# Cross-attention with its score products on 64-row halves of the array, and scores and values issued in one step

## The chip, the cores and the metric

The kernel runs on one core of a Trainium2 chip. The metric is the time of one execution in microseconds of the device. All data are fp32; some operands are held as fp32r, a form that TensorE multiplies in one pass.

## What is computed

A decoder of two layers over 32 sequences of 112 tokens (width 256), with a context of 375 tokens (width 192) for each sequence. Each layer has a self-attention block, a cross-attention block and a mixture of experts; x is normalised ahead of each and the result is added to it. The change touches the cross-attention of both layers, which is, for layer 0:

```python
q = x @ Wq.T + bq                       # 16 heads of 16
k = context @ Wk.T + bk
v = context @ Wv.T + bv
attn = jnp.einsum('bihd,bjhd->bhij', q, k) * SCALE
attn = jax.nn.softmax(attn, axis=-1)
out = jnp.einsum('bhij,bjhd->bihd', attn, v)
out = out.reshape(B, NQ, IN_DIM)
return out @ Wo.T + bo
```

Layer 1 has no product with Wo: out is added to x as it is.

## The kernel before

The stages run one after the other, with a barrier between them. `cross_attention` is called once for each layer. It goes through 8 groups of 4 sequences, and through each sequence in 4 units of 4 heads; a group has 16 units. The first and the last group are written out, the six between are one loop on every engine.

**Operands.** Each head has 16 numbers, and q and k are each held as a high and a low part in fp32r, so the product of one head needs 64 rows: q stands there as high, high, low, low and k against it as high, low, high, low. `kP` holds a pair of heads in one piece of 128 rows, head k of the pair (k is 0 or 1) on rows 64k to 64k + 63. `qP[:, s, k]` is the query of head k alone: its own 64 rows are filled by DMA, and the 64 of the other head are zeros, set once by POOL. So a product over 128 rows gives the scores of one head. One more column of k holds an identity, from which the row is shifted later.

**A unit u** goes through these steps, each on the engine named:
- `score` (PE, L1276), for each of its 2 pairs: two matmuls, 112 queries x 376, each into a bank of its own (0 and 1 for pair 0, 2 and 3 for pair 1). It waits until the maxima of the same pair of the unit before are read.
- `neg_max` (DVE, L1495), for each pair: the negative row maxima out of two banks.
- `make_diag` (POOL, L1433): the maxima of the 4 heads as diagonals.
- `exponent` (PE, L1290 and L1292), in 3 steps c = 0, 1, 2 of 125 context tokens each: the maxima are put in (L1290), and then the scores are computed again, turned (two matmuls of L1292). It writes bank 4 or 5 in turns, and waits until the exponential of the step two before is done.
- `exp` (ACT, L1389): one exponential for each step.
- `values` (PE, L1308): 12 matmuls (24 records) on 32-column parts of the array, 3 for each of the 4 heads, into bank 6.
- `copy_o4` (ACT, L1397): bank 6 to memory; the values of the next unit wait for it.

**The order** is written out by hand on every engine. Step i of a group is step c = i mod 3 of unit i // 3, and step `at` = i mod 12 of its sequence. Scores run two units ahead (`AHEAD`). On PE the steps before are: exponent, then a score pair of unit u + 2 (c = 0 and 1) or the values of unit u - 1 (c = 2). The jobs of a sequence are put behind the step that the table `AT` names: "xT" (two transposes of the normalised x, L1252, copied by ACT, L1382), "q" (the projection, L1258, which waits for that copy; then DVE splits it and DMA lays it out), "back" (four transposes of a finished sequence's output, L1321, then DVE divides by the row sums), and in layer 0 "oT" (two transposes, L1329, copied by ACT, L1402) and "y" (the product with Wo, L1335, which waits for that copy). All of them use bank 7, one after the other. ACT and DVE go through the same steps with their own part of each.

```python
    AT = {"xT": 1, "q": 2, "back": 4, "oT": 7, "y": 8}
```

Of the kernel before, what the change touches and what calls it, by code (L numbers as in the profile page):

```python
# [20 lines left out]
P = 128  # L21
EPS = 1e-5
GROUP = 4
ONE = 1
# [1077 lines left out]
def cross_attention(e, layer):  # L1102

    nc, sem, psum, bank, x, mv, rstd, ident, d = e.nc, e.sem, e.psum, e.bank, e.x, e.mv, e.rstd, e.ident, e.d
    T, D, B, NG, KD, H, HD = e.T, e.D, e.B, e.NG, e.KD, e.XH, e.XD
    KB, NJ, NKV = e.KB, e.NJ, e.NKV
    HU, SU, HALF = e.XU, e.SU, e.HALF
    a = e.xa[layer]
    n_ = f"x{layer}_"
    ST = (bank[4], bank[5])  # L1110
    PV, JOB = bank[6], bank[7]
    NU = GROUP * SU
    SS = SU * NJ
    VW, VH = P // HU, e.VH
# [2 lines left out]
    F32R = mybir.dt.float32r  # L1117
    AHEAD = 2
    RING = 4
    AT = {"xT": 1, "q": 2, "back": 4, "oT": 7, "y": 8}  # L1120
    SLOT = {at: j for j, at in AT.items()}
    MAKE = ("xT", "q")

    with ExitStack() as st:
# [14 lines left out]
        qP = sb("qP", [P, GROUP, 2, PAIRS, T], F32R)  # L1139
        kP = sb("kP", [P, 2, PAIRS, NKV + 1], F32R)  # L1140
# [8 lines left out]
        if layer == 0:  # L1149
            oT = sb("oT", [P, KD, T])  # L1150
# [8 lines left out]
        s_ps, max_done, diag_ready = count("scores_ps"), count("max_done"), count("diag_ready")  # L1159
# [5 lines left out]
        def since(g, per_group, n):  # L1165

            return max(g * per_group + n, 0) if type(g) is int else g * per_group + n
# [9 lines left out]
        with nc.Block() as block:  # L1177
# [62 lines left out]
            def _(pe):  # L1240
# [18 lines left out]
                                                 xnT[:, k, :], start=(k == 0), stop=(k == KD - 1))  # L1259
                        last.then_inc(q_ps, 1)  # L1260

                def score(g, u, pair):

                    if u >= NU:
                        g, u = g + 1, u - NU
                    s, q = divmod(u, SU)
                    r = s % 2
                    n = 2 * u + pair
                    if pair == 0 and q % 2 == 0:
                        pe.wait_ge(k_loaded[q // 2][r], g * (32 * GROUP) + 64 * (s // 2 + 1))  # L1270
                    if pair == 0 and q == 0:
                        pe.wait_ge(q_loaded[s], g * 128 + 128)

                    pe.wait_ge(max_done, ONE + since(g, 2 * NU, n - 1))
                    for k in range(2):
                        last = pe.matmul(bank[2 * pair + k][0:T, 0:NKV + 1], qP[:, s, k, 2 * q + pair, :],  # L1276
                                         kP[:, r, 2 * q + pair, :], start=True, stop=True)
                    last.then_inc(s_ps, 1)

                def exponent(g, i):  # L1280
                    u, c = divmod(i, NJ)
# [2 lines left out]
                    if c == 0:  # L1284
                        pe.wait_ge(diag_ready, ONE + g * NU + u + 1)

# [51 lines left out]
                def group(g, is_first, last):  # L1338
                    for i in range(NU * NJ):
                        u, c = divmod(i, NJ)  # L1340
                        s, at = divmod(i, SS)
                        more = s < GROUP - 2 or not last
                        exponent(g, i)
                        if c < 2 and (u + AHEAD < NU or not last):
                            score(g, u + AHEAD, c)
                        if c == 2 and (u > 0 or not is_first):
                            values(g, u - 1)
                        j = SLOT.get(at)
                        if j in MAKE and more:
                            job(g, s + 2, j)  # L1350
                        if s >= 1 or not is_first:
                            if j == "back":
                                turn_back(g, s - 1, more)
                            if j == "oT" and layer == 0:
                                turn_out(g, s - 1)
                            if j == "y" and layer == 0:
                                project(g, s - 1)
                    if last:
                        values(g, NU - 1)
                        turn_back(g, GROUP - 1, False)  # L1360
                        if layer == 0:
                            turn_out(g, GROUP - 1)
                            project(g, GROUP - 1)
# [3 lines left out]
                        job(0, s, j)  # L1367
                pe.wait_ge(made, 2)
                for u in range(AHEAD):
                    for pair in range(2):  # L1370
                        score(0, u, pair)
                all_groups(pe, group)

            @block.scalar
            def _(act):
                e.make_rstd_act(act, std_ready, std_asked, e.norm_tmp)

                def copy_xT(g, s):
                    b = g * GROUP + s
                    act.wait_ge(xT_ps, ONE + b + 1)  # L1380
                    act.wait_ge(q_ps, ONE + b)
                    act.activation(xnT[:].rearrange("p k t -> p (k t)"), JOB[:, 0:KD * T],  # L1382
                                   ACT.Copy).then_inc(xT_ready, 1)

                def exp(g, i):
                    u, c = divmod(i, NJ)
                    act.wait_ge(st_ps, ONE + g * (NU * NJ) + i + 1)
                    act.wait_ge(pv_ps, ONE + since(g, NU, u - 1))
                    act.activation(probT[:, u % 2, c].rearrange("k h t -> k (h t)"), ST[i % 2][0:KB, 0:HU * T],  # L1389
                                   ACT.Exp).then_inc(exp_done, 1)  # L1390

                def copy_o4(g, u):

                    s, q = divmod(u, SU)
                    act.wait_ge(pv_ps, ONE + g * NU + u + 1)
                    act.wait_ge(back_ps, ONE + since(g, GROUP, s - 1))
                    act.activation(o4T[:, s % 2, q, :], PV[:, 0:T], ACT.Copy).then_inc(o4_ready, 1)  # L1397

                def copy_oT(g, s):
                    act.wait_ge(oT_ps, ONE + g * GROUP + s + 1)  # L1400
                    act.wait_ge(y_ps, ONE + since(g, GROUP, s))
                    act.activation(oT[:].rearrange("p k t -> p (k t)"), JOB[:, 0:KD * T],  # L1402
                                   ACT.Copy).then_inc(oT_ready, 1)

                def group(g, is_first, last):
                    for i in range(NU * NJ):
                        u, c = divmod(i, NJ)
                        s, at = divmod(i, SS)
                        exp(g, i)
                        if c == 0 and (u > 1 or not is_first):  # L1410
                            copy_o4(g, u - 2)
                        j = SLOT.get(at)
                        if j == "xT" and (s < GROUP - 2 or not last):
                            copy_xT(g, s + 2)
                        if j == "oT" and layer == 0 and (s >= 1 or not is_first):
                            copy_oT(g, s - 1)
                    if last:
                        copy_o4(g, NU - 2)
                        copy_o4(g, NU - 1)
                        if layer == 0:  # L1420
                            copy_oT(g, GROUP - 1)

                for s in range(2):
                    copy_xT(0, s)
                all_groups(act, group)
# [39 lines left out]
            def _(dve):  # L1465
# [26 lines left out]
                def neg_max(g, u, pair):  # L1492
                    n = 2 * u + pair
                    dve.wait_ge(s_ps, ONE + g * (2 * NU) + n + 1)
                    dve.tensor_reduce(mx[:, u % RING, 2 * pair:2 * pair + 2], psum[0:T, 2 * pair:2 * pair + 2, 0:NKV],  # L1495
                                      AX_X, ALU.max, negate=True).then_inc(max_done, 1)
# [26 lines left out]
                def group(g, is_first, last):  # L1523
                    for i in range(NU * NJ):
                        u, c = divmod(i, NJ)
                        s, at = divmod(i, SS)
                        more = s < GROUP - 2 or not last
                        if at == 0 and more:
                            norm_x(g, s + 2)
                        if c < 2 and (u + AHEAD < NU or not last):  # L1530
                            neg_max(g, u + AHEAD, c)
                        j = SLOT.get(at)
                        if j == "q" and more:
                            split_q(g, s + 2)
                        if s >= 1 or not is_first:
                            if j == "back":
                                normalise(g, s - 1)
                            if j == "y" and layer == 0:
                                add_y(g, s - 1)
                    if last:  # L1540
                        normalise(g, GROUP - 1)
                        if layer == 0:
                            add_y(g, GROUP - 1)
# [892 lines left out]
```

## Time and profile before

| | |
|---|---|
| median of 3 runs | 3142.16 us (3135.05 to 3143.45) |
| profiled execution | 3136.99 us |
| its span | 3135.2 us, 58175 instructions |
| PE, DVE, ACT, POOL busy | 88%, 48%, 36%, 20% of the span |
| first and last start of L1276 | 747.1 and 2698.4 us |

The span is the time from the first to the last instruction; the execution's own time has a little around it. Matmuls are pipelined and overlap, so a sum of their durations is more than the time they take; what one of them takes of TensorE is read from the starts. The two stages of cross-attention lie from about 750 to 1210 us and from 2290 to 2710 us.

### The profile page before, as it was taken

What the parts mean: (1) busy time and instruction counts of PE and PEld (TensorE: products, weight loads), DVE (VectorE), ACT (ScalarE), POOL (GpSimd) and SP (SyncE); (2) the same over time, 40 slices, a digit from 0 to 9 for tenths busy, and PEclk for the clock granted to TensorE, in tenths of its full rate; (3) what the DMA queues carried; (4) which work ended last, traced back from release to release, by engine and by line L of the source; (5) the groups of instructions that cost most, each with busy time, mean ns of one, the idle gap of its engine ahead of it and who ended that gap; (6) DMA issues with size and microseconds to landing.
All of it is one profiled execution on the core that took longest, in us unless ns stands there. A gap on an engine that the chain in (4) does not pass through costs nothing. (4 is left out here: it accounts for less than half of the span.)

```text
span 3135.2 us, 58175 instructions
## 1 busy us (share of the span) xinstructions
PE 2746.9 (88%) x19352; PEld 2247.6 (72%) x19352; DVE 1498.8 (48%) x3187; ACT 1113.3 (36%) x2348; POOL 638.5 (20%) x660
## 2 busy tenths in 40 slices
PE   4999994996999998499999969899789999849992
PEld 2767672674888887488888857666578888848882
DVE  3455556335767664500000036555567777553334
ACT  1222235332555553033333324332145555402220
POOL 0000000003333331022222200000143333104542
PEclk8899996997999997599999989999889999859996
DMA  5000001786777772255655668600168888415666
GB/s 135 23 23 22 22 22 31 245 283 164 191 189 190 188 191 66 67 176 177 207 178 194 202 195 296 224 1 1 42 157 210 204 204 205 111 35 183 206 212 195
DMA packets 284132, 459.92 MB, mean 147 GB/s; under 512 B 73234, under 2 KB 211956, under 8 KB 284004
## 3 DMA queue, kind: packets, MB, share of 16 engines
q1 hardware_dynamic: 267236, 408.97, 46.0%
q0 software_dynamic: 16768, 49.30, 4.8%
q8 instruction: 72, 1.18, 0.2%
q14 instruction: 56, 0.46, 0.0%
HBM read 339.13 MB, written 119.02 MB: 146 GB/s over the span
## 5 line engine op out<-in xcount | busy, mean ns | idle before, releaser
L1389 ACT ACTIVATE x_probT<-banks 125x448 f32<-125x448 f32 x768 | 418.0, 544 | 402.3 <-PE banks L1292 392.6
L1495 DVE TENSOR_REDUCE x_neg_max<-banks 112x2 f32<-112x750 f32 x512 | 455.8, 931 | 97.7 <-PE banks L1276 97.7
L2000 PE MATMUL banks<-f_xT,f_w 128*128 128x256 f32 (+1 forms) x1680 | 368.7, 376 | 24.5 <-DMA f_b<-in_L_ffn_b 9.7
L2000 PEld LDWEIGHTS banks<-f_xT,f_w 128*128 128x128 f32 x1680 | 310.0, 196 | 76.6 <-issue 11.6
L1433 POOL TENSOR_TENSOR x_diag<-ident,x_neg_max 112x448 fp32r<-112x448 f32 x256 | 240.8, 941 | 575.4 <-DVE x_neg_max L1495 553.5
L2012 PE MATMUL banks<-f_w,f_hT 128*128 128x256 f32 x1584 | 354.3, 380 | 0.0
L1290 PE MATMUL banks<-x_diag,x_ones 112*125 112x448 f32 x768 | 324.5, 423 | 10.5 <-POOL x_diag L1433 9.8
L2012 PEld LDWEIGHTS banks<-f_w,f_hT 128*128 128x128 f32 x1584 | 296.2, 191 | 37.5
L1292 PEld LDWEIGHTS banks<-x_qP,x_kP 128*125 128x125 f32 x1536 | 291.3, 190 | 14.9
L1292 PE MATMUL banks<-x_qP,x_kP 128*125 128x224 f32 x1536 | 291.5, 271 | 0.0
L1276 PE MATMUL banks<-x_kP,x_qP 128*112 128x376 f32 x1024 | 264.5, 341 | 10.4 <-DMA x_qP<-q_halves 9.6
L2059 DVE TENSOR_TENSOR f_y<-banks,f_b 128x256 f32<-128x256 f32 x66 | 25.1, 420 | 478.2 <-PE banks L2012 478.2
L1940 POOL DMA_INDIRECT y_rows<-f_y,f_goes x132 | 131.2, 994 | 463.7 <-DVE f_y L2059 338.3
L2034 ACT ACTIVATE f_hT<-banks,f_b 128x256 f32<-128x256 f32 (+1 forms) x280 | 126.0, 461 | 219.7 <-PE banks L2000 202.2
L1308 PE MATMUL banks<-x_probT,x_v 125*32 125x112 f32 x6144 | 200.5, 263 | 0.8 <-ACT x_o4T L1397 0.8
L1931 POOL DMA_INDIRECT f_x_slots<-x_rows,f_came x132 | 130.2, 986 | 250.2 <-POOLq L101 198.7
L1290 PEld LDWEIGHTS banks<-x_diag,x_ones 112*125 112x125 f32 x768 | 143.8, 187 | 41.9 <-ACT x_probT L1389 22.0
L1308 PEld LDWEIGHTS banks<-x_probT,x_v 125*32 125x32 f32 x6144 | 138.7, 109 | 30.2 <-ACT x_o4T L1397 1.2
L1276 PEld LDWEIGHTS banks<-x_kP,x_qP 128*112 128x112 f32 x1024 | 147.9, 180 | 12.8 <-issue 10.1
L2037 ACT ACTIVATE f_hT<-banks 128x256 f32<-128x256 f32 (+1 forms) x140 | 52.0, 371 | 189.4 <-PE banks L2000 188.4
L949 PE MATMUL banks<-p_ctxT,x_wk_by_head 128*128 128x375 f32 x256 | 91.3, 501 | 27.2 <-DMA p_ctxT<-in_ctx_T 20.4
L2051 DVE TENSOR_TENSOR f_hT<-f_hT 128x256 f32<-128x256 f32 (+1 forms) x140 | 57.4, 410 | 90.7 <-ACT f_hT L2037 89.3
(321 smaller groups left out, 4096.7 us busy)
## 6 DMA issues: line engine op xcount, KB each, us to landing
x_kP<-k_halves SPq DMA_DIRECT2D x512, 188.0 KB, 3.6
f_w<-in_L_ffn_w SPq DMA_DIRECT2D x70, 1024.0 KB
f_w<-in_L_ffn_w SPq DMA_DIRECT2D x70, 512.0 KB
x_qP<-q_halves SPq DMA_DIRECT2D x512, 56.0 KB, 3.2
x_v<-v_rows SPq DMA_DIRECT2D x64, 408.0 KB, 3.2
k_halves<-p_halves SPq DMA_DIRECT2D x32, 752.0 KB, 3.6
k_halves<-f_d_halves SPq DMA_DIRECT2D x32, 752.0 KB, 4.0
q_halves<-x_q_halves SPq DMA_DIRECT2D x64, 224.0 KB, 2.3
```

Source lines behind the costliest of these rows:

```text
L1276: last = pe.matmul(bank[2 * pair + k][0:T, 0:NKV + 1], qP[:, s, k, 2 * q + pair, :], kP[:, r, 2 * q + pair, :], start=True, stop=True)
L1290: pe.matmul(to, ones[:], diag[:, u % RING].rearrange("t h k -> t (h k)"), start=True, stop=False)
L1292: last = pe.matmul(to[:, 2 * pair * T:2 * (pair + 1) * T].rearrange("k (h t) -> k h t", t=T), kP[:, r, 2 * q + pair, keys], qP[:, s, :, 2 ...
L1308: last = pe.matmul(PV[j * VW:(j + 1) * VW, 0:T], v[0:KB, s % 2, at:at + VW], probT[:, u % 2, c, j, :], start=(c == 0), stop=(c == NJ - 1))
L1389: act.activation(probT[:, u % 2, c].rearrange("k h t -> k (h t)"), ST[i % 2][0:KB, 0:HU * T], ACT.Exp).then_inc(exp_done, 1)
L1433: pool.tensor_tensor(diag[:, u % RING], wide(ident[0:T, 0:T].unsqueeze(1), 1, HU), wide(mx[:, u % RING, :].unsqueeze(2), 2, T), ALU.mult). ...
L1495: dve.tensor_reduce(mx[:, u % RING, 2 * pair:2 * pair + 2], psum[0:T, 2 * pair:2 * pair + 2, 0:NKV], AX_X, ALU.max, negate=True).then_inc( ...
L1931: pool.indirect_dma_start(out=x_slots[:, n % 2, j, :], out_offset=None, in_=e.x_rows, in_offset=bass.IndirectOffsetOnAxis(ap=came[:, at:at ...
L1940: pool.indirect_dma_start(out=e.y_rows, out_offset=bass.IndirectOffsetOnAxis(ap=goes[:, at:at + 1], axis=0), in_=y[:, n % 2, j, :], in_off ...
L2000: last = pe.matmul(bank[1 + f % 3][:, 0:width], w1[:, r, k, f * P:(f + 1) * P], xT[:, r, k, 0:width], start=(k == 0), stop=(k == KD - 1))
L2012: last = pe.matmul(bank[4 + 2 * r + j][:, 0:D], hT[:, f, j * P:(j + 1) * P], w2[:, r, f, :], start=(f == 0), stop=(f == NF - 1))
L2034: act.activation(hT[:, f, 0:width], bank[1 + f % 3][:, 0:width], ACT.Gelu, bias=b1[:, r, f:f + 1]).then_inc(h_raw, 1)
```

## The change

It has four parts. The score matmuls read 64 rows of q and k each (`ROWS[k]`) in place of 128, so that the two of a pair stand on different halves of the array's rows; the zeros of `qP` are still set, since `exponent` reads them. Both pairs of a unit are issued in one step, c = 1, and the values of unit u - 1 right behind them, in the same step. ACT's `copy_o4` of unit u - 1 moves to c = 2 of unit u, and DVE's maxima to c = 1 and 2. Each job moves one step later.

```diff
--- before.py
+++ after.py
@@ -1109,6 +1109,7 @@
     n_ = f"x{layer}_"
     ST = (bank[4], bank[5])
     PV, JOB = bank[6], bank[7]
+    ROWS = (slice(0, HALF), slice(HALF, P))
     NU = GROUP * SU
     SS = SU * NJ
     VW, VH = P // HU, e.VH
@@ -1117,7 +1118,7 @@
     F32R = mybir.dt.float32r
     AHEAD = 2
     RING = 4
-    AT = {"xT": 1, "q": 2, "back": 4, "oT": 7, "y": 8}
+    AT = {"xT": 2, "q": 3, "back": 5, "oT": 8, "y": 9}
     SLOT = {at: j for j, at in AT.items()}
     MAKE = ("xT", "q")
 
@@ -1259,23 +1260,23 @@
                                                  xnT[:, k, :], start=(k == 0), stop=(k == KD - 1))
                         last.then_inc(q_ps, 1)
 
-                def score(g, u, pair):
+                def scores(g, u):
 
                     if u >= NU:
                         g, u = g + 1, u - NU
                     s, q = divmod(u, SU)
                     r = s % 2
-                    n = 2 * u + pair
-                    if pair == 0 and q % 2 == 0:
+                    if q % 2 == 0:
                         pe.wait_ge(k_loaded[q // 2][r], g * (32 * GROUP) + 64 * (s // 2 + 1))
-                    if pair == 0 and q == 0:
+                    if q == 0:
                         pe.wait_ge(q_loaded[s], g * 128 + 128)
 
-                    pe.wait_ge(max_done, ONE + since(g, 2 * NU, n - 1))
-                    for k in range(2):
-                        last = pe.matmul(bank[2 * pair + k][0:T, 0:NKV + 1], qP[:, s, k, 2 * q + pair, :],
-                                         kP[:, r, 2 * q + pair, :], start=True, stop=True)
-                    last.then_inc(s_ps, 1)
+                    for pair in range(2):
+                        pe.wait_ge(max_done, ONE + since(g, 2 * NU, 2 * u + pair - 1))
+                        for k in range(2):
+                            last = pe.matmul(bank[2 * pair + k][0:T, 0:NKV + 1], qP[ROWS[k], s, k, 2 * q + pair, :],
+                                             kP[ROWS[k], r, 2 * q + pair, :], start=True, stop=True)
+                        last.then_inc(s_ps, 1)
 
                 def exponent(g, i):
                     u, c = divmod(i, NJ)
@@ -1341,9 +1342,9 @@
                         s, at = divmod(i, SS)
                         more = s < GROUP - 2 or not last
                         exponent(g, i)
-                        if c < 2 and (u + AHEAD < NU or not last):
-                            score(g, u + AHEAD, c)
-                        if c == 2 and (u > 0 or not is_first):
+                        if c == 1 and (u + AHEAD < NU or not last):
+                            scores(g, u + AHEAD)
+                        if c == 1 and (u > 0 or not is_first):
                             values(g, u - 1)
                         j = SLOT.get(at)
                         if j in MAKE and more:
@@ -1367,8 +1368,7 @@
                         job(0, s, j)
                 pe.wait_ge(made, 2)
                 for u in range(AHEAD):
-                    for pair in range(2):
-                        score(0, u, pair)
+                    scores(0, u)
                 all_groups(pe, group)
 
             @block.scalar
@@ -1407,15 +1407,14 @@
                         u, c = divmod(i, NJ)
                         s, at = divmod(i, SS)
                         exp(g, i)
-                        if c == 0 and (u > 1 or not is_first):
-                            copy_o4(g, u - 2)
+                        if c == 2 and (u > 0 or not is_first):
+                            copy_o4(g, u - 1)
                         j = SLOT.get(at)
                         if j == "xT" and (s < GROUP - 2 or not last):
                             copy_xT(g, s + 2)
                         if j == "oT" and layer == 0 and (s >= 1 or not is_first):
                             copy_oT(g, s - 1)
                     if last:
-                        copy_o4(g, NU - 2)
                         copy_o4(g, NU - 1)
                         if layer == 0:
                             copy_oT(g, GROUP - 1)
@@ -1527,8 +1526,8 @@
                         more = s < GROUP - 2 or not last
                         if at == 0 and more:
                             norm_x(g, s + 2)
-                        if c < 2 and (u + AHEAD < NU or not last):
-                            neg_max(g, u + AHEAD, c)
+                        if c >= 1 and (u + AHEAD < NU or not last):
+                            neg_max(g, u + AHEAD, c - 1)
                         j = SLOT.get(at)
                         if j == "q" and more:
                             split_q(g, s + 2)
```

The order of instructions shows it at two places. The first is on PE in layer 0, from the exponent with the jobs "xT" and "q" to the next values (the names are those of the tiles; L1290 and L1292 are an exponent, L1276 scores, L1308 values, L1252 xT, L1258 q). Before:

```order
L1276 MATMUL banks<-x_kP,x_qP 112x376 x2
L1252 MATMUL banks<-ident,x_xn 128x112 x2
L1290 MATMUL banks<-x_diag,x_ones 125x448
L1292 MATMUL banks<-x_qP,x_kP 125x224 x2
L1308 MATMUL banks<-x_probT,x_v 32x112 x12
L1258 MATMUL banks<-x_xnT,x_wq_by_head 128x112 x4
L1290 MATMUL banks<-x_diag,x_ones 125x448
L1292 MATMUL banks<-x_qP,x_kP 125x224 x2
L1276 MATMUL banks<-x_kP,x_qP 112x376 x2
```

And now, one line number further:

```order
L1253 MATMUL banks<-ident,x_xn 128x112 x2
L1291 MATMUL banks<-x_diag,x_ones 125x448
L1293 MATMUL banks<-x_qP,x_kP 125x224 x2
L1259 MATMUL banks<-x_xnT,x_wq_by_head 128x112 x4
L1291 MATMUL banks<-x_diag,x_ones 125x448
L1293 MATMUL banks<-x_qP,x_kP 125x224 x2
L1277 MATMUL banks<-x_kP,x_qP 112x376 x4
L1309 MATMUL banks<-x_probT,x_v 32x112 x12
```

Between xT and q stood an exponent and the values; now an exponent alone stands there, and the four scores are in one piece ahead of the values.

The second is PE between unit 3 of a sequence and unit 0 of the next, where no job is, now:

```order
L1277 MATMUL banks<-x_kP,x_qP 112x376 x4
L1309 MATMUL banks<-x_probT,x_v 32x112 x12
L1291 MATMUL banks<-x_diag,x_ones 125x448
L1293 MATMUL banks<-x_qP,x_kP 125x224 x2
L1291 MATMUL banks<-x_diag,x_ones 125x448
L1293 MATMUL banks<-x_qP,x_kP 125x224 x2
L1291 MATMUL banks<-x_diag,x_ones 125x448
L1293 MATMUL banks<-x_qP,x_kP 125x224 x2
L1277 MATMUL banks<-x_kP,x_qP 112x376 x4
L1309 MATMUL banks<-x_probT,x_v 32x112 x12
```

Three exponents follow each other here; before, every exponent had scores, values or a job behind it.

## Rows read from the trace of the kernel before

**Rows 1.** The page: engines' busy time; groups (busy, mean ns, idle before).
```profile
PE 2746.9 (88%) x19352; PEld 2247.6 (72%) x19352; DVE 1498.8 (48%) x3187; ACT 1113.3 (36%) x2348; POOL 638.5 (20%) x660
...
L1495 DVE TENSOR_REDUCE x_neg_max<-banks 112x2 f32<-112x750 f32 x512 | 455.8, 931 | 97.7 <-PE banks L1276 97.7
...
L1433 POOL TENSOR_TENSOR x_diag<-ident,x_neg_max 112x448 fp32r<-112x448 f32 x256 | 240.8, 941 | 575.4 <-DVE x_neg_max L1495 553.5
```

**Rows 2.** Busy time by stretch: us, PE, PEld, DVE, ACT, POOL, PEclk, DMA share, GB/s.
```profile
754.00:1195.00 441.00, 436.19 (x5202) 384.82 (x5201) 307.04 (x519) 242.66 (x560) 146.75 (x157) 0.99 0.74 181
2303.00:2707.00 404.00, 403.16 (x5082) 356.49 (x5081) 307.30 (x518) 232.60 (x531) 142.11 (x153) 1.00 0.81 195
```

**Rows 3.** Timeline of PE, 889.0 to 892.2 us: start, us until the group's end.
```profile
888.83 0.49 PE L1321 MATMUL banks<-ident,x_o4T 128*112 128x128 f32 x3
...
889.36 0.38 PE L1292 MATMUL banks<-x_qP,x_kP 128*125 128x224 f32 x2
889.67 0.78 PE L1308 MATMUL banks<-x_probT,x_v 125*32 125x112 f32 x24
890.38 0.47 PE L1290 MATMUL banks<-x_diag,x_ones 112*125 112x448 f32 x1
...
890.90 0.50 PE L1276 MATMUL banks<-x_kP,x_qP 128*112 128x376 f32 x2
891.24 0.37 PE L1290 MATMUL banks<-x_diag,x_ones 112*125 112x448 f32 x1
891.44 0.38 PE L1292 MATMUL banks<-x_qP,x_kP 128*125 128x224 f32 x2
891.66 0.51 PE L1276 MATMUL banks<-x_kP,x_qP 128*112 128x376 f32 x2
```

**Rows 4.** Timeline of self-attention, 425.3 to 426.9 us.
```profile
425.37 0.55 PE L582 MATMUL banks<-ident,sa_prob 112*112 112x112 f32 x4
...
425.85 1.03 PE L573 MATMUL banks<-sa_kT,sa_qT 64*112 64x112 f32 x8
...
426.81 0.68 PE L560 MATMUL banks<-w_v,sa_xnT 128*112 128x512 f32 x1
```

**Rows 5.** Timeline of the last units of layer 1, 2700 to 2716 us.
```profile
2703.06 0.47 PE L1290 MATMUL banks<-x_diag,x_ones 112*125 112x448 f32 x1
...
2703.58 0.38 PE L1290 MATMUL banks<-x_diag,x_ones 112*125 112x448 f32 x1
...
2703.78 0.54 ACT L1389 ACTIVATE x_probT<-banks 125x448 f32<-125x448 f32 x1 [0.78 <-PE banks L1292]
...
2704.22 0.26 ACT L1397 ACTIVATE x_o4T<-banks 128x112 f32<-128x112 f32 x1
2704.36 0.55 ACT L1389 ACTIVATE x_probT<-banks 125x448 f32<-125x448 f32 x1
...
2704.38 0.47 PE L1290 MATMUL banks<-x_diag,x_ones 112*125 112x448 f32 x1 [0.20 <-ACT x_probT L1389]
...
2705.00 0.78 PE L1308 MATMUL banks<-x_probT,x_v 125*32 125x112 f32 x24
```

**Rows 6.** Timeline of layer 0, 884.0 to 888.7 us.
```profile
884.77 0.36 PE L1252 MATMUL banks<-ident,x_xn 112*128 112x112 f32 x2
...
884.90 0.45 PE L1290 MATMUL banks<-x_diag,x_ones 112*125 112x448 f32 x1
...
885.19 0.37 PE L1292 MATMUL banks<-x_qP,x_kP 128*125 128x224 f32 x2
...
888.16 0.38 PE L1292 MATMUL banks<-x_qP,x_kP 128*125 128x224 f32 x2
888.27 0.28 PEld L1276 LDWEIGHTS banks<-x_kP,x_qP 128*112 128x112 f32 x2
```

**Rows 7.** Timeline of the first sequence of layer 1, 2270.6 to 2272 us.
```profile
2271.28 0.36 ACT L1382 ACTIVATE x_xnT<-banks 128x224 f32<-128x224 f32 x1 [2.59 <-PE banks L1252]
2271.69 0.50 PEld L1258 LDWEIGHTS banks<-x_xnT,x_wq_by_head 128*128 128x128 f32 x2 [0.79 <-ACT x_xnT L1382]
```

## The prediction

> **What bounds the kernel now.** I read the page first, for each engine's share of the span and for the granted clock, then the busy time of each engine over the two stretches of cross-attention, then the timeline inside them, instruction by instruction. PE is busy for 88% of the whole span [rows 1], and in the two cross-attention stages for 436.19 of 441 us and 403.16 of 404 us, at a granted clock of 0.99 and 1.00, while DVE stands at 307 and ACT at 243 and 233 us [rows 2]. So in these stages nothing else is late: what TensorE issues, and how long it stands still, is the time. "Busy" hides pieces, though, since matmuls overlap; the starts on the timeline show what each piece really takes from TensorE [rows 3]. An exponent step (the max term, L1290, and two products of L1292) takes 0.42 us to the next start (891.24 to 891.66). A score step of two matmuls, L1276, takes 0.34 us (890.90 to 891.24), 0.17 us each. The values (24 records of L1308) take 0.71 us (889.67 to 890.38), and the exponent behind them takes 0.52 us in place of 0.42 (890.38 to 890.90). There are 16 units in a group, 8 groups and 2 layers: 256 units, or 64 sequences of 4 units.
>
> **Part 1, the scores on half the array.** A unit has four score matmuls, 4 x 0.17 = 0.67 us in sequence. Now the two of a pair stand on rows 0 to 63 and 64 to 127 and write different banks. The trace of before has no two matmuls on different rows, so I bound this: at worst they still follow each other (0), at best the second costs nothing. The nearest row is L1308, where four matmuls on different columns of the array run together: 24 of them start within 0.78 - 0.26 = 0.52 us [rows 3], 0.26 being the length of one, so a matmul beside another is nearly free. I take the best: 2 x 0.168 x 256 = **-86 us**. The moving side still has 376 columns, so the two that are left are not shorter.
>
> **Part 2, one more change of the array's shape per unit.** Before, a unit goes from the full array to 32-column parts and back. Now it goes from the full array to 64-row halves, from there to the 32-column parts, and back. The last two are there already. Self-attention shows what a step onto 64 rows costs [rows 4]: the last of four L582 starts at 425.37 + 0.55 - 0.26 = 425.66, the last of eight L573 (64 rows, 112 columns) at 425.85 + 1.03 - 0.26 = 426.62; eight steps of 0.098 us would be 0.78, and it is 0.96. I take +0.18 us, 256 times: **+46 us**. Bounds: 0 if halves and parts cost no more than one change does, and 0.36 if the step into the values costs as much too (+92). The Trainium skill (TensorEngine Tiling (Array Packing), Key Properties) says that a change of tiling mode drains TensorE, even though a change of tile within a mode does not; the trace agrees, by those 0.18 us. A rule that speaks against the change stands in the Trainium skill (TensorE: Matmul & The Clock Gate, Part 3): a weight load runs under matmuls in flight only on other rows. By it the second pair's loads, on the same rows as the first pair's matmuls, would stand bare, an estimated 0.09 us a unit or 23 us more.
> The row speaks otherwise: the load of L1276 begins at 888.27, on all rows, while the L1292 matmuls that began at 888.16 on all rows run for 0.38 us [rows 6]. I go by the row.
>
> **Part 3, exponents without cover.** There are two banks for exponents, so each waits for the ACT exponential of the exponent two before it. Before, a score step or the values lay between any two. Now a unit's c = 2 and the next unit's c = 0 and c = 1 follow each other, with only a job between at most. The last units of a layer have no scores ahead of them and show just this [rows 5]: exponents at 2703.06, 2703.58 and 2704.38. The third starts 0.80 us after the second, not 0.42; it had to wait for the exponential that ran from 2703.78 for 0.54 us. It then takes 0.62 us to the values, against 0.42 + 0.10 for the same step without a wait (from the first L1292 to the values 0.31 us, 889.36 to 889.67, where 0.21 is usual [rows 3]), because its weight load now stands bare. The price is 0.38 + 0.10 = 0.48 us. It falls due where no job stands between: in layer 0 once a sequence (unit 3 to unit 0; the others have back, xT, q, oT or y), in layer 1 twice (there is no oT and no y). (32 + 64) x 0.48 = **+46 us**. Bounds: 0 if every such place is covered, +123 if it fell due in all 256 units. The shortest job there, the four turns of "back" at 0.11 us each (888.83: three in 0.49, one being 0.27 long [rows 3]), covers the 0.38 just about.
>
> **Part 4, q waits for its own transpose.** Before, the transposes xT and the projection q had an exponent and the values between them, over 1.1 us. Now there is one exponent. On ACT the copy of xT stands behind the exponential of the same step and the copy o4. From the start of the exponent behind the values: its exponential starts at +0.72 (2703.06 to 2703.78 [rows 5]), the o4 copy 0.44 later and whatever follows that 0.14 later (2703.78, 2704.22, 2704.36 [rows 5]), the copy of xT takes 0.36 and the weight load starts 0.05 after its end (2271.28 + 0.36 to 2271.69 [rows 7]). Together 1.71 us. TensorE itself is there after 0.52 + 0.21 + 0.42 = 1.15 us, 0.21 being xT (884.77 to 884.90, and L1292 0.29 behind that L1290 [rows 6], where 0.20 is usual [rows 3]). It waits 0.56 us, and 0.10 for the bare load (L1290 takes 0.47 in place of 0.37 in such a place [rows 3]): 0.66 us, 60 times within the groups, **+40 us**. Bounds: 0.52 if the o4 copy costs nothing, 0.88 if exponential and o4 copy take their whole 0.54 and 0.26 one after the other.
>
> **Part 5, y waits for oT.** The same chain in the same places (c = 2 and c = 0) of layer 0, 31 times: 0.66 x 31 = **+20 us**.
>
> **What costs nothing.** On DVE the maxima move one step later with their scores. DVE has 307 us of work in 441 [rows 2], and the next unit's scores come over 3 us later (441 us for 128 units), against 2 x 0.89 us for both maxima (L1495, 455.8 us for 512 [rows 1]). The diagonal of POOL, 0.94 us, is needed a whole unit later. If that cover went, each unit would wait for the rest. The o4 copy comes a little earlier, which the next values don't need. SP's queue keeps its order; it waits for exponents and values, and those keep their order too.
>
> **The sum**: -86 + 46 + 46 + 40 + 20 = **+66 us**. The profiled execution took 3136.99 us (span 3135.2), so 3203; on the median of the runs, 3142.16, it gives **3208 us**. About 0.3% is what a measurement of this kernel can tell from no change.
>
> **The rivals.**
> *Waits covered (faster).* The place is ACT: if its chain ran ahead far enough, parts 3 to 5 would vanish and -86 + 46 = -40 stays: 3102. It decides from a point: the 106 us of waits must fall under 40, some 0.2 us for each of 187 places in place of 0.48 to 0.66. For it: ACT is idle 45% of the stage [rows 2]. Against it: rows 5 show the wait in the very order that the change makes the rule. Chance 0.13.
> *The halves follow each other.* Two matmuls on different rows take turns: part 1 gives 0, and +152 makes 3294. For it: no row shows such a pair; against it: the parts of L1308. Chance 0.08.
> *The change doesn't do what it says:* operands on 64 partitions but run as on the full array. No gain and no change of shape, waits alone: +106, 3248. L573 with its 0.18 us speaks against. Chance 0.06.
> *Bare loads under the second pair,* the rule above, worked out as a mechanism: 0.09 us more, half of the 0.18 us that self-attention pays for draining and a bare load together [rows 4], in 256 units, +23: 3231. It speaks against it that full-row loads run beside full-row matmuls [rows 6]. Chance 0.04.
> *The clock.* With pauses in TensorE the granted clock, 0.99 and 1.00 here, could fall to 1.2 GHz for a part of the stage. A tenth of 845 us at half speed would add 84: 3292. Against: the pauses are under 1 us each, and TensorE still works some 90% of the time. Chance 0.05.
>
> **How the numbers follow.** The forecast has 0.64, and its own range is 3175 to 3240, from the bounds of parts 2 and 4. The range of 8 in 10 takes in the third and fourth rivals and part of the second and fifth: 3150 to 3280; the faster rival (0.13) and about half of the slow ones stay outside. Faster: the first rival, and the low edge of the forecast with several terms off at once, 0.14. Within 0.3% (3133 to 3152): 0.05. Slower: 0.81.
>
> **What would show it.** In the profile of the changed kernel the second score matmul of a pair starts less than 0.02 us after the first, and the four take about 0.34 us between two starts in place of 0.67, with 0.2 more ahead of the first. TensorE is idle ahead of the q projection for ACT's copy of xT, about 0.5 us each; ahead of the y projection the same in layer 0; and ahead of the third exponent in a row, for ACT's x_probT, some 0.2 us of idle TensorE and 0.4 us of idle weight load, 96 times. PE's busy time in the two stretches falls while they get longer, layer 0 by 1.2 us a sequence and layer 1 by 1.0. If the four scores take 0.67 us, part 1 is wrong; if the waits on ACT come to less than 40 us, parts 3 to 5 are.

## The result and the profile after

| | before | changed |
|---|---|---|
| median, measured together | 3141.72 us (4 runs, 3135.05 to 3143.45) | 3208.49 us (4 runs, 3205.33 to 3213.09) |
| profiled execution | 3136.99 us | 3210.14 us |
| its span | 3135.2 us | 3208.4 us |

The ratio is 1.0218, with a 95% interval of 1.0206 to 1.0230: slower by 67 us. The forecast was 3208 us, +66.

The page of the changed kernel, answering to [rows 1] (columns as there):

```profile
PE 2765.2 (86%) x19352; PEld 2172.5 (68%) x19352; DVE 1498.4 (47%) x3187; ACT 1083.4 (34%) x2348; POOL 638.4 (20%) x660
...
L1494 DVE TENSOR_REDUCE x_neg_max<-banks 112x2 f32<-112x750 f32 x512 | 454.9, 930 | 122.4 <-PE banks L1277 122.4
```

Busy time by stretch, answering to [rows 2] (us, then PE, PEld, DVE, ACT, POOL, granted clock, DMA share, GB/s):

```profile
754.00:1230.00 476.00, 441.65 (x5164) 345.89 (x5164) 305.47 (x517) 223.76 (x555) 145.88 (x156) 0.99 0.69 168
2330.00:2770.00 440.00, 410.68 (x5018) 318.40 (x5018) 314.02 (x519) 217.42 (x527) 151.89 (x156) 0.99 0.75 181
```

PE now stands still for 34 of 476 us and for 29 of 440 us, where it stood still for 5 and 1. DVE has the work it had and ACT nearly so (1083 us busy in place of 1113), in more time. The granted clock is 0.99 in both stretches, where it was 0.99 and 1.00.

The timeline of PE between unit 3 of a sequence and unit 0 of the next, in layer 0 (exponents, then scores and values), answering to [rows 3] and [rows 5]:

```profile
954.99 0.47 PE L1291 MATMUL banks<-x_diag,x_ones 112*125 112x448 f32 x1
...
955.50 0.37 PE L1291 MATMUL banks<-x_diag,x_ones 112*125 112x448 f32 x1
...
956.30 0.47 PE L1291 MATMUL banks<-x_diag,x_ones 112*125 112x448 f32 x1 [0.21 <-ACT x_probT L1389]
956.61 0.38 PE L1293 MATMUL banks<-x_qP,x_kP 128*125 128x224 f32 x2
956.91 0.60 PE L1277 MATMUL banks<-x_kP,x_qP 64*112 64x376 f32 x4
957.44 0.78 PE L1309 MATMUL banks<-x_probT,x_v 125*32 125x112 f32 x24
```

The four scores and the step into the values take 0.53 us (956.91 to 957.44), and the last exponent ahead of them reaches their start 0.30 us after its first L1293 (956.61 to 956.91) where 0.21 was usual. The inside of the slot, first the weight loads of all four scores (PEld), then the matmuls that run between 956.92 and 957.15 us, which are the first pair and the L1293 ahead of it:

```profile
956.91 0.27 PEld L1277 LDWEIGHTS banks<-x_kP,x_qP 64*112 64x112 f32 x4
```

```profile
956.71 0.27 PE L1293 MATMUL banks<-x_qP,x_kP 128*125 128x224 f32 x1
956.91 0.43 PE L1277 MATMUL banks<-x_kP,x_qP 64*112 64x376 f32 x2
```

By the records of the trace the four matmuls start at 956.911, 956.915, 957.177 and 957.181: the second of the first pair 3 to 4 ns after the first, in every one of the 256 slots, and the second pair 0.26 us after the first pair. The second pair's loads run from 957.01 to 957.18, beside the first pair's matmuls, which use the same rows.

The three exponents start at 954.99, 955.50 and 956.30: 0.51 and then 0.80 us apart, as in the last units of the kernel before, and the third needs 0.61 us to the scores.

The stretch with xT and q, all engines, answering to [rows 6] and [rows 7]:

```profile
958.46 0.38 PE L1293 MATMUL banks<-x_qP,x_kP 128*125 128x224 f32 x2
...
958.67 0.36 PE L1253 MATMUL banks<-ident,x_xn 112*128 112x112 f32 x2
...
958.80 0.45 PE L1291 MATMUL banks<-x_diag,x_ones 112*125 112x448 f32 x1
958.88 0.55 ACT L1389 ACTIVATE x_probT<-banks 125x448 f32<-125x448 f32 x1 [1.31 <-PE banks L1293]
...
959.09 0.38 PE L1293 MATMUL banks<-x_qP,x_kP 128*125 128x224 f32 x2
959.32 0.26 ACT L1397 ACTIVATE x_o4T<-banks 128x112 f32<-128x112 f32 x1
...
959.46 0.36 ACT L1382 ACTIVATE x_xnT<-banks 128x224 f32<-128x224 f32 x1
...
959.88 1.15 PE L1259 MATMUL banks<-x_xnT,x_wq_by_head 128*128 128x112 f32 x8 [0.41 <-ACT x_xnT L1382]
```

The exponent behind the values starts ACT's exponential at 958.88; o4 follows at 959.32, 0.44 later, the copy of xT at 959.46, 0.14 later, and q starts at 959.88, 0.06 after the copy's end. From the L1293 ahead of it q is 0.79 us away (959.09 to 959.88), where 0.21 is usual: 0.58 us.

The waits of PE in the middle of layer 0 and then of layer 1 (who waited for whom, us in total, times, longest):

```profile
PE banks L1259 <- ACT x_xnT L1382: 11.6, 28, 0.4
PE banks L1336 <- ACT x_oT L1402: 11.5, 28, 0.4
PE banks L1291 <- ACT x_probT L1389: 5.9, 28, 0.2
```

```profile
PE banks L1291 <- ACT x_probT L1389: 11.5, 55, 0.2
PE banks L1259 <- ACT x_xnT L1382: 11.2, 27, 0.4
```

One third exponent a sequence in layer 0 and two in layer 1, one q in both, one y in layer 0: the list of parts 3 to 5. And the step from one copy of xT to the next, which is one sequence (timeline of ACT, layer 0 and then layer 1):

```profile
959.46 0.36 ACT L1382 ACTIVATE x_xnT<-banks 128x224 f32<-128x224 f32 x1
...
974.68 0.36 ACT L1382 ACTIVATE x_xnT<-banks 128x224 f32<-128x224 f32 x1
```

```profile
2506.13 0.36 ACT L1382 ACTIVATE x_xnT<-banks 128x224 f32<-128x224 f32 x1
...
2520.11 0.36 ACT L1382 ACTIVATE x_xnT<-banks 128x224 f32<-128x224 f32 x1
```

Over 28 steps of layer 0 the mean is 15.24 us, where it was 14.03; over 27 steps of layer 1 it is 13.99, where it was 12.94. In these same steps PE's busy time went from 392.75 to 397.64 us and from 349.42 to 355.10 us, and its idle time from nothing to 28.9 and 22.5 us.

### The profile page after: what moved, and what is told of

It reads as the page before. It is cut to its first block and busy times, and to the rows that moved or that the text cites. A ratio compares the mean times of both kernels' runs of the same rounds, so it can differ in the third digit from the quotient of the medians.

```text
span 3208.4 us, 58367 instructions
## 1 busy us (share of the span) xinstructions
PE 2765.2 (86%) x19352; PEld 2172.5 (68%) x19352; DVE 1498.4 (47%) x3187; ACT 1083.4 (34%) x2348; POOL 638.4 (20%) x660
## 5 line engine op out<-in xcount | busy, mean ns | idle before, releaser
L1291 PE MATMUL banks<-x_diag,x_ones 112*125 112x448 f32 x768 | 348.4, 454 | 28.1 <-ACT x_probT L1389 20.4
L1293 PEld LDWEIGHTS banks<-x_qP,x_kP 128*125 128x125 f32 x1536 | 292.4, 190 | 15.4
L1293 PE MATMUL banks<-x_qP,x_kP 128*125 128x224 f32 x1536 | 292.1, 272 | 0.0
L1277 PE MATMUL banks<-x_kP,x_qP 64*112 64x376 f32 x1024 | 156.9, 383 | 12.3 <-DMA x_qP<-q_halves 10.1
L1277 PEld LDWEIGHTS banks<-x_kP,x_qP 64*112 64x112 f32 x1024 | 71.2, 174 | 43.9 <-issue 11.5
L1259 PE MATMUL banks<-x_xnT,x_wq_by_head 128*128 128x112 f32 x512 | 77.7, 298 | 26.1 <-ACT x_xnT L1382 26.1
```

The source lines that it names most:

```text
L1277: last = pe.matmul(bank[2 * pair + k][0:T, 0:NKV + 1], qP[ROWS[k], s, k, 2 * q + pair, :], kP[ROWS[k], r, 2 * q + pair, :], start=True, st ...
L1291: pe.matmul(to, ones[:], diag[:, u % RING].rearrange("t h k -> t (h k)"), start=True, stop=False)
L1293: last = pe.matmul(to[:, 2 * pair * T:2 * (pair + 1) * T].rearrange("k (h t) -> k h t", t=T), kP[:, r, 2 * q + pair, keys], qP[:, s, :, 2 ...
```

## The experiments

Each run stands beside a time of the kernel before that was taken with it, on the same chip. "Over before" is the difference of the two medians; for the changed kernel it is +66.8.

**Full rows again.** The order as changed, the score matmuls back on 128 rows.

```diff
-    ROWS = (slice(0, HALF), slice(HALF, P))
+    ROWS = (slice(0, P), slice(0, P))
```

> The changed kernel with ROWS full for both: each score matmul on all 128 rows again, order as changed. Theory (part 1 is -86 us, part 2 is +46 us): undoing both gives +40, 3248 us. If the halves bring nothing (part 1 is 0), it gives -46, 3162. If the change of shape costs nothing (part 2 is 0), +86, 3294.

Measured: 3248.36 us, before 3137.90, ratio 1.0352 (1.0336 to 1.0367), +110.5 over before, so 44 more than the changed kernel. Its timeline of PE:

```profile
1000.70 0.38 PE L1293 MATMUL banks<-x_qP,x_kP 128*125 128x224 f32 x2
1000.91 0.85 PE L1277 MATMUL banks<-x_kP,x_qP 128*112 128x376 f32 x4
1001.69 0.78 PE L1309 MATMUL banks<-x_probT,x_v 125*32 125x112 f32 x24
1002.40 0.49 PE L1291 MATMUL banks<-x_diag,x_ones 112*125 112x448 f32 x1
```

From the scores' start to the values it is now 0.78 us (1000.91 to 1001.69) where the halves take 0.53: 0.25 us saved. The step ahead of them is 0.21 us (1000.70 to 1000.91) where it is 0.30: 0.09 lost. Net 0.16 us a unit, 256 units, 41 us. The parts -86 and +46 have about the right sum (-40 forecast); the next run weighs them otherwise, since it pays for the change of shape twice as often.

**Halves in the old order.** The kernel before, with this alone:

```diff
-                        last = pe.matmul(bank[2 * pair + k][0:T, 0:NKV + 1], qP[:, s, k, 2 * q + pair, :],
-                                         kP[:, r, 2 * q + pair, :], start=True, stop=True)
+                        last = pe.matmul(bank[2 * pair + k][0:T, 0:NKV + 1], qP[k * HALF:(k + 1) * HALF, s, k, 2 * q + pair, :],
+                                         kP[k * HALF:(k + 1) * HALF, r, 2 * q + pair, :], start=True, stop=True)
```

> The kernel before with the 64-row halves alone, its order untouched. Each of 512 pairs then pays a step onto 64 rows (0.18 us) and one back (0.18 to 0.21) and saves 0.17: +0.21 x 512 = +107, 3249 us, with no wait on ACT. If only one shape change costs anything, 3142 + 0.01 x 512 = 3147. If neither costs anything, -86, 3056.

Measured: 3240.26 us, before 3137.90, ratio 1.0332 (1.0316 to 1.0348), +102.4. Its timeline of PE:

```profile
1001.17 0.37 PE L1292 MATMUL banks<-x_qP,x_kP 128*125 128x224 f32 x2
1001.48 0.42 PE L1276 MATMUL banks<-x_kP,x_qP 64*112 64x376 f32 x2
1001.83 0.47 PE L1290 MATMUL banks<-x_diag,x_ones 112*125 112x448 f32 x1
1002.14 0.38 PE L1292 MATMUL banks<-x_qP,x_kP 128*125 128x224 f32 x2
```

The two matmuls on different halves last 0.42 us together, as long as each of them by itself (median 419 ns), so they do run together. But the exponent's L1292 is followed after 0.31 us (1001.17 to 1001.48) in place of 0.21, the next L1290 after 0.35 us, and its own L1292 again after 0.31 us in place of 0.20. Summed over these three steps that is 0.97 in place of 0.75 us; by the medians it is 102.4 / 512 = 0.20 us a pair, and where the remaining 0.02 goes was not followed. So a pair saves 0.17 us and pays 0.37. From 760 to 1200 us PE waits nowhere for ACT. The halves pay only where one change of shape serves several matmuls, which speaks for putting both pairs beside the values. No run has both pairs together but away from the values; by these figures it would save 0.34 us and pay 0.37, an estimate.

**Both low, then both high.** The changed kernel with the loops over `pair` and `k` exchanged in `scores`:

```diff
-                    for pair in range(2):
-                        pe.wait_ge(max_done, ONE + since(g, 2 * NU, 2 * u + pair - 1))
-                        for k in range(2):
+                    for k in range(2):
+                        for pair in range(2):
+                            if k == 0:
+                                pe.wait_ge(max_done, ONE + since(g, 2 * NU, 2 * u + pair - 1))
...
```

> The changed kernel with its four scores in another order: both of rows 0 to 63, then both of rows 64 to 127. Theory (two matmuls run together only if they are neighbours on different rows, and start in order): three steps of 0.168 us in place of two, +43, 3251 us. Rival (halves do not overlap, and the gain comes from elsewhere): 3208. Rival (the array takes any of the four that is free): 3208 too, and then the starts of the matmuls tell them apart.

Measured: 3210.18 us, before 3136.19, ratio 1.0239 (1.0224 to 1.0255), +74.0, 7 above the changed kernel's +66.8 and not 43. The medians themselves, 3210.18 and 3208.49 us, and the intervals of the ratios don't tell the two apart. The theory that the four start in the order of the program fell. Timeline of PE:

```profile
957.04 0.38 PE L1295 MATMUL banks<-x_qP,x_kP 128*125 128x224 f32 x2
957.35 0.60 PE L1278 MATMUL banks<-x_kP,x_qP 64*112 64x376 f32 x4
957.88 0.78 PE L1311 MATMUL banks<-x_probT,x_v 125*32 125x112 f32 x24
```

The slot is 0.53 us long (957.35 to 957.88), as before. The next run marks the halves.

**Halves marked.** The same, with 376 columns for rows 0 to 63 and 374 for rows 64 to 127:

```diff
...
+                            cols = NKV + 1 - 2 * k
-                            last = pe.matmul(bank[2 * pair + k][0:T, 0:NKV + 1], qP[ROWS[k], s, k, 2 * q + pair, :],
-                                             kP[ROWS[k], r, 2 * q + pair, :], start=True, stop=True)
+                            last = pe.matmul(bank[2 * pair + k][0:T, 0:cols], qP[ROWS[k], s, k, 2 * q + pair, :],
+                                             kP[ROWS[k], r, 2 * q + pair, 0:cols], start=True, stop=True)
```

> As the run with both scores of rows 0 to 63 issued first, then both of rows 64 to 127, but the matmuls on rows 64 to 127 read 374 columns in place of 376, so that the trace tells the halves apart (the last token is left out of the second head's maximum, which only shifts that head's exponents). Theory (each half of the array takes its own matmuls in order, past those that wait for the other half): of the two that start together one has 376 columns and one 374, in both pairs. Rival (in order, and two on the same rows run together): the first two starts have 376 columns both. The time stays near 3210 in both.

One execution: 3208.66 us. The program issues 376, 376, 374, 374. Groups by form in a window that ends before the third matmul starts (1000.80 to 1000.95 us):

```profile
L1279 PE MATMUL banks<-x_kP,x_qP 64*112 64x374 f32 x1 | 0.4, 422 | 0.0
L1279 PE MATMUL banks<-x_kP,x_qP 64*112 64x376 f32 x1 | 0.4, 421 | 0.0
```

And in a window from 1001.10 to 1001.35 us, which all four touch:

```profile
L1279 PE MATMUL banks<-x_kP,x_qP 64*112 64x376 f32 x2 | 0.6, 376 | 0.0
L1279 PE MATMUL banks<-x_kP,x_qP 64*112 64x374 f32 x2 | 0.6, 374 | 0.0
```

Of the two that start first, one has 376 and one 374 columns. So a matmul on the free half started ahead of one that the program has before it and that waited for its own half. The records of the whole execution say the same in 253 of its 256 slots: 376, 374, then about 0.26 us later 376, 374. In the other three, near the start of a stage, the second matmul of the program had to wait for DVE's maxima, and then the order is 376, 376, 374, 374:

```profile
749.21 0.65 PE L1279 MATMUL banks<-x_kP,x_qP 64*112 64x376 f32 x1 [1.00 <-DVE x_neg_max L1497]
750.05 0.97 PE L1279 MATMUL banks<-x_kP,x_qP 64*112 64x376 f32 x3 [0.19 <-DVE x_neg_max L1497]
```

Here a matmul of 374 columns had a free half from the start and did not start past the wait. So in this kernel the order was given up for a busy half and not for a wait on another engine; the three slots are all that show the second. The starts on the free half explain the time of the run before, and they say that part 1 doesn't depend on which two are neighbours.

**xT and oT one step earlier.**

```diff
-    AT = {"xT": 2, "q": 3, "back": 5, "oT": 8, "y": 9}
+    AT = {"xT": 1, "q": 3, "back": 5, "oT": 7, "y": 9}
```

> The changed kernel with the transposes xT and oT one step earlier (steps 1 and 7, behind the values), everything else the same, q and y where they are. Theory (parts 4 and 5, 60 us, are q and y waiting for ACT's copy): 3208 - 60 = 3148 us, no idle TensorE ahead of q and y, the waits of third exponents unchanged. Rival (the time is lost elsewhere, and those waits only take the place of others): stays at 3208.

Measured: 3146.43 us, before 3137.90, ratio 1.0024 (1.0013 to 1.0035), +8.5: 58 us less than the changed kernel, where 60 were expected. What is left is parts 1 to 3, +6 by the forecast. In the waits of PE in layer 0 (760 to 1200 us) q and y are gone from the list, and the third exponents stay, 0.2 us each:

```profile
PE banks L1291 <- ACT x_probT L1389: 6.9, 33, 0.2
```

**ACT's copies in the other order.** The changed kernel, in ACT's `group`: `copy_xT` and `copy_oT` ahead of `copy_o4`.

```diff
-                        if c == 2 and (u > 0 or not is_first):
-                            copy_o4(g, u - 1)
                         j = SLOT.get(at)
...
                             copy_oT(g, s - 1)
+                        if c == 2 and (u > 0 or not is_first):
+                            copy_o4(g, u - 1)
```

> The changed kernel with ACT's copies of xT and oT ahead of its o4 copy in the same step. Theory (the chain of parts 4 and 5: exponential, 0.44 us, o4 copy, 0.14 us, copy, projection): the copy starts 0.14 us earlier, 91 times, -13 us, 3195. Rival (ACT takes longer from an exponential to this copy, 0.54 us as before the change): -4, 3204.

Measured: 3193.94 us, before 3139.11, ratio 1.0177 (1.0160 to 1.0194), +54.8: 12 less than the changed kernel's, where 13 were expected. Its timeline in the same place:

```profile
955.17 0.55 ACT L1389 ACTIVATE x_probT<-banks 125x448 f32<-125x448 f32 x1 [1.31 <-PE banks L1293]
...
955.61 0.35 ACT L1382 ACTIVATE x_xnT<-banks 128x224 f32<-128x224 f32 x1
...
955.85 0.27 ACT L1397 ACTIVATE x_o4T<-banks 128x112 f32<-128x112 f32 x1
...
956.02 1.15 PE L1259 MATMUL banks<-x_xnT,x_wq_by_head 128*128 128x112 f32 x8 [0.26 <-ACT x_xnT L1382]
```

The copy of xT starts 0.44 us after the exponential, and q 0.06 us after the copy's end. The chain has the links that part 4 gave it.

**Jobs spread.**

```diff
-    AT = {"xT": 2, "q": 3, "back": 5, "oT": 8, "y": 9}
+    AT = {"xT": 1, "q": 3, "back": 5, "oT": 8, "y": 11} if layer == 0 else {"xT": 2, "q": 5, "back": 8}
```

> The changed kernel with the jobs spread so that nearly every pair of exponents without scores between has one: layer 0 xT 1, q 3, back 5, oT 8, y 11, layer 1 xT 2, q 5, back 8. Theory: parts 4 and 5 gone (-60), and of part 3's 96 waits of 0.48 us some 33 us are left (one partly covered in layer 0, one whole and one partly covered in layer 1), -13: 3135 us, 7 below the kernel before. Rival (more waits on DVE or the bank the jobs share appear): 3150 or more.

Measured: 3135.66 us (11 runs), before 3137.90 (18 runs), ratio 0.9992 (0.9983 to 1.0001), -2.2, where -7 was expected. The new work on the array and the old time, near enough: 69 us, of 106 forecast for the waits, were a matter of where five small jobs stand.

**Jobs split.** The projection q of layer 1 in two halves, by output rows, and y of layer 0 in two halves, by its two products, each half with a place of its own (the new table alone is shown, the split of the two jobs is left out):

```diff
...
+    AT = {"xT": 1, "q": 3, "back": 5, "oT": 7, "ya": 9, "y": 11} if layer == 0 else {"xT": 1, "qa": 3, "q": 5, "back": 8}
```

> The changed kernel with its jobs spread and two of them split so that they cover more places: layer 0 xT 1, q 3, back 5, oT 7, the first half of y 9, the second 11; layer 1 xT 1, the first half of q 3, the second 5, back 8. Theory: no wait is left in layer 0, and one of 0.48 us a sequence in layer 1 (15 us): -86 + 46 + 15 = -25 on the kernel before, 3113 us beside the 3138 that it took in the last comparison. Rival (halving a job opens a wait on the bank that the jobs share, or leaves a bare load each time): 3130 or more.

Measured: 3122.52 us, before 3136.19, ratio 0.9962 (0.9948 to 0.9975), -13.7: 0.4% faster than the kernel before, and 11 us short of the 25 expected. By the profile the mean step of a sequence is 13.41 us in layer 0 and 12.86 in layer 1, where the kernel before had 14.03 and 12.94, so over 32 sequences layer 0 gave the 20 us that it should and layer 1 some 3 where 5 were due. The other 9 us stay open: whether they come from the first and last sequences of a stage or from other stages is not known. Single runs of one kernel here lie up to 13 us apart.

**xT of layer 1 between two exponents.** As the last, with this (the two lines that keep layer 0 and the first sequences as they were are left out):

```diff
-{"xT": 1, "qa": 3, "q": 5, "back": 8}
+{"xT": 0, "qa": 3, "q": 5, "back": 8}
...
+                        if at == 10 and layer and (s + 3 < GROUP or not last):
+                            norm_x(g, s + 3)
```

> As the run with split jobs, and in layer 1 DVE's normalising of x two steps earlier and xT at step 0, so that 0.21 us of work stand in the last bare place. Theory: the wait there falls from 0.38 to 0.17 us, with the bare load still to pay: -0.21 x 32 = -7 on that run, 3106. Rival (DVE is late there with x, or with the maxima behind it): no gain or a loss.

Measured: 3125.38 us, before 3136.19, ratio 0.9962 (0.9948 to 0.9976), where 3106 was expected: no gain on the run with split jobs. Waits of PEld in layer 1 (2400 to 2600 us), first of the run with split jobs, then of this one:

```profile
PEld banks L1293 <- ACT x_probT L1395: 6.3, 16, 0.4
```

```profile
PEld banks L1279 <- DVE x_neg_max L1500: 5.1, 15, 0.4
PEld banks L1293 <- ACT x_probT L1395: 3.3, 15, 0.2
```

The wait for the exponential fell from 0.39 to 0.22 us each, as meant, but the scores now wait for DVE's maximum, 0.34 us each: the normalising of x now stands ahead of it on DVE. That is the rival, a new wait in the place of the old.

## Why the prediction was right

The mechanism is the one forecast: the halves save the second matmul of each pair, and lost cover over ACT's latency costs more than that. The terms agree with the runs one by one, to within some 6 us each:

- **What bounds the kernel.** Right: TensorE had no idle time to give, so every wait showed in full, and so did all that the halves saved.
- **Parts 1 and 2** (-86 and +46, net -40). The run with full rows gives -44 by the medians and -41 by the timeline, the halves in the old order +102 where +107 was expected. The second matmul of a pair is free, as taken from the 32-column parts (it starts 3 to 4 ns after the first), and the step onto 64 rows, measured on self-attention, holds: 0.09 us ahead of the scores, and 0.09 more between the first pair's start and the second's, 0.26 us in place of 0.17. The sign named for it was off in its place: of the "0.2 more ahead of the first" only half lies ahead. The upper bound of part 2, a dearer step into the values, did not come about: with full rows the last score matmul starts 0.26 us ahead of the values, as the second pair does with halves.
- **Part 3** (+46). The third exponent starts 0.80 us after the second and takes 0.61 us, against 0.80 and 0.62 in [rows 5]; it falls due 28 times beside 28 projections q in the layer 0 list, and 55 times beside 27 in layer 1's. The run with xT and oT early leaves +8.5 for parts 1 to 3; with -44 for the first two, part 3 is about 52.
- **Parts 4 and 5** (+40 and +20). Moving xT and oT takes away 58 of 60 us, and the chain on ACT has the links 0.44, 0.14, 0.36 and 0.06. What was too high is a detail: PE's idle time ahead of q is 0.41 us, not "about 0.5", since the matmul ahead still runs for a part of the 0.58.
- **The rivals.** "Waits covered" did not happen: the waits stand in the lists above. "The halves follow each other" and "not done as said" are excluded by the starts and by the run with full rows. Bare loads under the second pair are excluded by the rows of the loads: all four loads end 0.27 us after the first began, and the second pair's run beside matmuls on the same rows. The clock did not fall: 0.99.
- **The steps of a sequence** came out as forecast: 1.21 us more in layer 0 (1.2 forecast) and 1.05 in layer 1 (1.0).
- **PE's busy time** is one sign that came out the other way. It was to fall in the two stretches; over the same sequences it rose by 4.9 and 5.7 us. The forecast's own figures don't give a fall either: its waits of 0.5 and 0.2 us of idle TensorE come to some 65 us, about all of the +66. A bare load and the pause at a change of shape stand in the busy time (a score matmul of the first pair lasts 0.42 us, where one on full rows lasts 0.33), so what the halves saved was filled up again in this count.
- **The range.** 3175 to 3240 was said to come from the bounds of parts 2 and 4, but part 2 alone at its bounds gives 3162 or 3254. It was drawn tighter than that, and the result did not test it.
- **The sum** agrees to within 1 us (+66 forecast, +66.8 measured), which is better than its terms are known and partly luck: by the runs they are about -44, +52 and +58, so errors of -4, +6 and -2 cancel.

## What to carry to other kernels

Putting matmuls on row halves saves the second one whole, but each visit costs a pause and a bare weight load on both sides: 0.37 us here against 0.17 us saved a pair, so gather several pairs, and if possible beside work that changes the array's shape anyway. When pieces of work are gathered into one slot, look at what they were covering where they stood: here 0.34 us of scores between two exponents hid ACT's latency, and the lost cover, there and ahead of q and y, cost about 2.5 times the net gain of some 40 us. Most of it comes back when small jobs are moved into the bare places, but each moved job can open a wait of its own, as the last run shows on DVE. The last iterations of a loop, where a stage runs dry, can show beforehand what an order without the cover costs, as they did here.

## What was not expected of the hardware

TensorE started a matmul on the free half of the rows ahead of one that stands before it in the program and whose half was busy: issued as 376, 376, 374, 374 columns, the first two starts were a 376 and a 374 in 253 of 256 slots, and the four took 0.53 us to the values in either order. In the three slots where the second one waited for DVE, none started past it. The Trainium skill (TensorE: Matmul & The Clock Gate, Part 3) says that matmuls start and end in the order of the program; for these four on two halves the trace shows otherwise.
